# Second attention: score matmuls for the row maxima in the full array shape, between a slot's two score blocks

## The reference

```python
q = (x @ W_dq.T @ W_uq.T).reshape(B, T, nh, hs).transpose(0, 2, 1, 3)   # 16 heads of 8
q_lat = jnp.einsum('bhtd,hdl->bhtl', q, k_eff)
attn = jnp.einsum('bhtl,bsl->bhts', q_lat, c_kv) / math.sqrt(hs)
attn = jnp.where(causal_mask, -jnp.inf, attn)       # key after query: left out
attn = jax.nn.softmax(attn, axis=-1)
ctx = jnp.einsum('bhts,bsl->bhtl', attn, c_kv)
```

## Time and profile before

| what | us |
|---|---|
| three runs, median (lowest, highest) | 2035.82 (2034.11, 2042.33) |
| the profiled execution, first to last instruction (span) | 2036.8 |
| second attention, prelude: first maximum to first score block | 1305.2 to 1337.9 |
| its units 0 to 7, first score block to the end | 1337.9 to 1666 |
| experts of the last layer | 1666 to 2036.8 |

### The profile page before, as it was taken

The page is one execution under the profiler, slowest core; times in us unless marked ns, Lnnn a source line. Parts: engine busy times, 40 slices in busy tenths (PEclk is TensorE's granted clock), DMA queues, the critical chain, the costliest instruction groups (busy, mean ns, idle before and its releaser), DMA issues. The chain is left out here.

```text
span 2036.8 us, 32306 instructions
## 1 busy us (share of the span) xinstructions
PE 1760.2 (86%) x10685; PEld 757.0 (37%) x10685; DVE 1468.9 (72%) x1473; ACT 1323.0 (65%) x2673; POOL 886.3 (44%) x567
## 2 busy tenths in 40 slices
PE   7779999999786777776776699899999999999996
PEld 2313333333344444444443333334444444233332
DVE  3678888887399999999999754556666624465456
ACT  4427777777799999989999534335555553543432
POOL 1076556664299999999999710000000001000000
PEclk8759999999998888888889899879999988999997
DMA  2354444442698888888888411322223000000000
GB/s 108 133 176 162 156 157 151 152 161 110 209 321 315 304 297 312 309 281 314 301 306 300 158 53 48 62 56 56 40 47 58 18 18 0 0 0 0 0 6 16
DMA packets 86546, 288.88 MB, mean 142 GB/s; under 512 B 11671, under 2 KB 15026, under 8 KB 84383
## 3 DMA queue, kind: packets, MB, share of 16 engines
q1 hardware_dynamic: 72319, 236.57, 36.3%
q0 software_dynamic: 13824, 50.34, 6.4%
q10 hardware_dynamic: 288, 0.45, 0.1%
HBM read 214.60 MB, written 61.21 MB: 135 GB/s over the span
## 5 line engine op out<-in xcount | busy, mean ns | idle before, releaser
L565 DVE TENSOR_REDUCE attn_mx<-banks 128x1 f32<-128x1024 f32 (+7 forms) x512 | 501.7, 990 | 148.0 <-PE banks L363 98.4
L1648 POOL TENSOR_TENSOR hc<-st,ct 128x1024 f32<-128x1024 f32 x256 | 597.7, 2368 | 6.4 <-DVE st L1607 6.0
L1607 DVE TENSOR_TENSOR_SCAN st<-da,banks 128x1024 f32<-128x1024 f32 x256 | 562.5, 2266 | 15.6 <-ACT da L1564 6.0
L517 ACT ACTIVATE attn_probs<-banks 128x512 f32<-128x512 f32 (+3 forms) x640 | 307.2, 533 | 193.8 <-PE banks L397 100.2
L1572 ACT ACTIVATE ut<-b_turned,mats 128x128 f32<-128x128 f32 x1024 | 311.6, 387 | 1.7
L1564 ACT ACTIVATE da<-dt,mats 128x1024 f32<-128x1024 f32 x256 | 282.6, 1138 | 25.3 <-DVE st L1607 18.6
L393 PE MATMUL banks<-attn_qa,attn_ka 75*128 75x512 bf16 (+3 forms) x896 | 268.9, 369 | 4.5 <-DMA attn_qa<-attn_mrow 2.5
L1489 PE MATMUL banks<-hc,onecol 128*32 128x512 f32 x1024 | 158.9, 696 | 102.1 <-POOL onecol L1646 79.6
L743 POOL TENSOR_TENSOR made_ahead<-b_turned,x_turned 128x1024 f32<-128x1024 f32 x96 | 183.8, 1914 | 110.9 <-DVE attn_mparts L580 59.1
L361 PE MATMUL banks<-attn_ka,attn_qa 64*128 64x512 bf16 (+3 forms) x512 | 197.1, 385 | 25.1 <-DVE attn_mx L565 21.0
L1465 PE MATMUL banks<-mats,ut 128*128 128x128 f32 x1024 | 162.5, 300 | 45.2 <-DVE st L1607 34.2
(11 more groups left out here) (442 smaller groups left out, 1977.9 us busy)
## 6 DMA issues: line engine op xcount, KB each, us to landing
dt<-dt_rows SPq DMA_DIRECT2D x256, 512.0 KB, 5.5
ahead<-made_ahead POOLq DMA_DIRECT2D x96, 512.0 KB, 3.4
ua<-ahead SPq DMA_DIRECT2D x96, 512.0 KB, 5.9
attn_qa<-q_lin SPq DMA_DIRECT2D x144, 64.0 KB
attn_qu<-attn_qa SPq DMA_DIRECT2D x16, 512.0 KB, 4.3
attn_ka<-k_lin SPq DMA_DIRECT2D x72, 64.0 KB
moe_w<-in_moe_w SPq DMA_DIRECT2D x2, 2048.0 KB, 11.5
mats<-in_mats SPq DMA_DIRECT2D x1, 2876.5 KB, 13.0
```

The source lines that it names most:

```text
L517: nc.scalar.activation(probs[s % 4][:, jj, c0:BLK], scores_exp[jj][:, c0:BLK], ACT.Exp, scale=scale).then_inc(probs_ready, 1)
L565: nc.vector.reduce_max(mx[:, qt, j:j + 1], scores_max[n % 2][:, 0:w], AX.X)\
L1607: nc.vector.tensor_tensor_scan(st[n % 4][:, :], da[n % 4][:, :], pair[:, :, :].rearrange("p h t -> p (h t)"), 0.0, ALU.mult, ALU.add).then ...
L1648: nc.gpsimd.tensor_tensor(hc[n % 8][:, :], st[n % 4][:, :], ct[:, b * SEQ:(b + 1) * SEQ], ALU.mult)\
```

## The change

`qu`, `ku`, the semaphore `mirrored` and the two DMAs of `mirror` fall away for the causal call. `max_unit` takes all 72 rows of `qa` and `ka` for all keys, so that a maximum of more than 512 keys is two matmuls from the same rows; the first one of a unit waits for `loaded` in place of `mirrored`, and so does the load of unit i for the transfers of unit i-2 on the same semaphore. `exp_unit` can make one of its two blocks; in `body` the maxima of place 2s come between the slot's two score blocks. The places, the maxima in them and place 2s+1 stay. The first layer's attention keeps all of this as it was.

```diff
--- before.py
+++ after.py
@@ -159,8 +159,9 @@
     with ExitStack() as ctx:
         qa = [k.sb(f"{tag}_qa{i}", [128, 4, SEQ], BF16, ctx) for i in range(RING)]
         ka = [k.sb(f"{tag}_ka{i}", [128, nk, SEQ], BF16, ctx) for i in range(RING)]
-        qu = [k.sb(f"{tag}_qu{i}", [128, 4, SEQ], BF16, ctx) for i in range(2)]
-        ku = [k.sb(f"{tag}_ku{i}", [128, nk, BLK], BF16, ctx) for i in range(2)]
+        if not causal:
+            qu = [k.sb(f"{tag}_qu{i}", [128, 4, SEQ], BF16, ctx) for i in range(2)]
+            ku = [k.sb(f"{tag}_ku{i}", [128, nk, BLK], BF16, ctx) for i in range(2)]
         probs = [*probs, *(k.sb(f"{tag}_probs{i}", [128, 2, BLK], F32, ctx) for i in range(4 - len(probs)))]
         mx = k.sb(f"{tag}_mx", [128, QT, 4], F32, ctx)
         mneg = k.sb(f"{tag}_mneg", [128, QT, 4], F32, ctx)
@@ -223,7 +224,7 @@
         done_half = [slot_of((1, first_half - 1)), slot_of((0, NM - 1))]
 
         loaded = [k.sem(f"{tag}_loaded{i}") for i in range(2)]
-        mirrored = [k.sem(f"{tag}_mirrored{i}") for i in range(2)]
+        mirrored = None if causal else [k.sem(f"{tag}_mirrored{i}") for i in range(2)]
         const_ready = k.sem(f"{tag}_const")
         ones_set = k.sem(f"{tag}_ones_set")
         ones_in = [k.sem(f"{tag}_ones_in{i}") for i in range(RING)]
@@ -273,6 +274,8 @@
                             .then_inc(ones_in[i], 16)
                     elif p == 0:
                         sp.wait_ge(exp_scored, 2 * NE * (i - RING + 1))
+                    if causal and i >= 2 and p == 0:
+                        sp.wait_ge(loaded[i % 2], 18 * 16 * (i // 2))
                     for j in range(9):
                         if K_ORDER[j] == p:
                             load_k(sp, i, j)
@@ -293,6 +296,8 @@
 
                 def mirror(i):
 
+                    if causal:
+                        return
                     sp.wait_ge(loaded[i % 2], 18 * 16 * (i // 2 + 1))
                     if i >= 2:
                         sp.wait_ge(max_taken, NM * (i - 1))
@@ -346,7 +351,9 @@
 
                 def max_unit(i, n):
                     qt, j, w = max_units[n]
-                    if n == 0:
+                    if n == 0 and causal:
+                        pe.wait_ge(loaded[i % 2], 18 * 16 * (i // 2 + 1))
+                    elif n == 0:
                         pe.wait_ge(mirrored[i % 2], 32 * (i // 2 + 1))
 
                     pe.wait_ge(max_taken, NM * i + max(n - 1, 0))
@@ -354,7 +361,9 @@
                     for lo in range(0, w, BLK):
                         hi = min(lo + BLK, w)
                         diag = causal and hi == w
-                        if lo == 0:
+                        if causal:
+                            lhs, rhs = qa[i % RING][0:ROWS, j, sl(qt, TILE)], ka[i % RING][0:ROWS, kj(j), lo:hi]
+                        elif lo == 0:
                             lhs, rhs = qa[i % RING][0:64, j, sl(qt, TILE)], ka[i % RING][0:64, kj(j), 0:hi]
                         else:
                             lhs, rhs = qu[i % 2][64:128, j, sl(qt, TILE)], ku[i % 2][64:128, kj(j), 0:hi - BLK]
@@ -376,15 +385,15 @@
                                                 ident_b[:, :], start=True, stop=True)
                     last.then_inc(mturned[half], 1)
 
-                def exp_unit(i, s):
+                def exp_unit(i, s, halves=(0, 1)):
                     qb, kt, hp, c0 = exp_units[s]
-                    if s == 0:
+                    if s == 0 and 0 in halves:
                         pe.wait_ge(mrow_sent[0], 48 * (i + 1))
                         if i < RING:
                             pe.wait_ge(ones_in[i], 16)
-                    if s == MID:
+                    if s == MID and 0 in halves:
                         pe.wait_ge(mrow_sent[1], 48 * (i + 1))
-                    for jj in range(2):
+                    for jj in halves:
                         if i > 0 or s > 0:
                             pe.wait_ge(probs_ready, 2 * (NE * i + s) + jj - 1)
                         j = 2 * hp + jj
@@ -455,8 +464,13 @@
                             products_with_v = None
                         if products_with_v:
                             pv_quad(*products_with_v, 0)
-                        first_pass(i, 2 * s)
-                        exp_unit(i, s)
+                        if causal:
+                            exp_unit(i, s, (0,))
+                            first_pass(i, 2 * s)
+                            exp_unit(i, s, (1,))
+                        else:
+                            first_pass(i, 2 * s)
+                            exp_unit(i, s)
                         if s == done_half[1] + 2:
                             turn_max(i, 1)
                         if s == done_half[0] + 2 and i + 1 < UNITS:
```

## The result

| | kernel before | changed kernel |
|---|---|---|
| runs, median (lowest, highest), us | 2035.4 (2034.11, 2042.33), 4 runs | 2017.77 (2014.9, 2020.24), 4 runs |
| span of the profiled execution, us | 2036.8 | 2018.4 (its own time 2020.24) |
| ratio of the times | | 0.9908, 95% interval 0.9878 to 0.9937 |

What follows compares the result with a forecast made beforehand. TensorE was taken to set the pace, with a low-clock stretch in unit 0. Terms -9.0 (units 1 to 6), -7 (unit 0), -1 (prelude), +0.3 (unit 7) gave -16.7 on 2036.8, a 2019 us median; range 2010 to 2031.

Steps and rivals of the forecast that it cites:

- Parts 1 and 2: Units 1 to 6: 51 fewer shape switches save 5.1 us a unit, second-half columns cost 2.2; net 2.9 less.
- part 3: Units 1 to 6: waits take back about 1.4 us a unit, leaving 38.9 each; -9.0 us for six.
- Part 4: Unit 0: clock still falls but recovers after a third to half of the stretch; -7 us (floor -3, ceiling -11).
- Part 6: Unit 7: three 1024-key maxima save 5 switches but pay more columns, and maximum 31 is later; +0.3 us.
- Part 5: Prelude: only some narrow maxima ahead of two front matmuls are on the path; -1 us (0 to -2).
- Part 8: Behind the attention: the experts' instructions are unchanged, though low clock may move; 0 us (-2 to +2).
- Part 7: Mirrors: dropping 16 issues on SyncE's queue costs and gains nothing, hidden by its idle time; 0 us (-0.5 to +0.5).
- A: Rival, unit 0: the low-clock stretch stays as long as now, its term only -3; 2023 us, chance 0.17.
- D: Rival, maxima: shape switches stay, so only the added columns count, 7 x 2.2 us; 2051 us, chance 0.02.
- B: Rival, units 1 to 6: slot 8's chain and VectorE's pace take back nearly all; 2028 us, chance 0.15.
- C: Rival, units 1 to 6: idle TensorE lets the clock fall, 9.5 us a fall; six give 2076; chance 0.10.

Runs made afterwards that it cites:

- 64-row kernel: Changed kernel with the maxima from the first 64 rows alone, for both halves of the keys; 2172.9 us, ratio 1.0687.
- 65-row one: Changed kernel with the maxima from 65 rows instead of 72; 2018.31 us, ratio 0.9891.
- second profile of before: Kernel before, unchanged, in the later of its two further profiles; 2035.78 us.
- first further profile of before: Kernel before, unchanged, profiled once more; 2037.08 us.
- run with the mirrors: Changed kernel with the two mirror copies of each unit issued again and waited for, but not read; 2022.18 us, ratio 0.9924.
- place-only kernel: Kernel before with only the maxima moved between the two score blocks, 64 rows and mirrors kept; 2059.78 us, ratio 1.0103.

## Why the prediction was right, and where a term was off

**Parts 1 and 2 (switches and columns), and part 3 (waits): right.** 38.9 us a unit was forecast, 38.73 measured, -9.9 for six units where -9.0 was forecast. By pieces: the start distances are the predicted ones (0.06 into a maximum, 0.43 for its two blocks of 512), and slots 14 to 17 are each 0.10 shorter (1.59 to 1.49, 1.71 to 1.61). The count of switches is the trace's, 100 and 49, and four single maxima of the 64-row kernel against the 65-row one give the price of a switch afresh, 0.10 us. The net of parts 1 and 2 can be checked roughly too: the 40.39 us of before, less 2.9 net and less the 0.96 of idle time, would be 36.5, and with the long waits taken away a unit takes 36.57 and 36.37, some 0.3 of it still idle ahead of maximum 0.

The waits by size: ahead of maximum 0 1.19 us where 1.3 were forecast (0.2 more than before, not 0.3); ahead of slot 8 0.64 us where 0.8 were; and the 0.2 of slot 10 is gone, since with the order of before the changed shape pays it again (1.34 us against 1.14). The 0.45 for slots 4 and 5 was a little short. From turning out the output to turning the maxima, a stretch with maxima 1 to 5 in both kernels, it is 3.58 us (1424.69 to 1428.27) where it was 3.94 (1435.22 to 1439.16): 0.36 of the 1.0 came, so 0.64 went into waits. Maximum 3 has most of it: it starts 0.52 behind a mask where 0.06 would do. With these sizes the sum closes: 2.9 less 0.2, 0.64 and 0.64, plus the 0.2 of slot 10, is 1.6 us a unit, and 1.66 came. The reading of the earlier trace rows, that this stretch could shrink by 0.34 us at most, held to the hundredth: 3.99 against 3.98.

**Part 4 (unit 0): the clock was rightly named as the source of the gain; its size was wrong.** Its -7 stood for "the clock still falls, and comes back after a third to half". It didn't fall: -12.0, past the ceiling of -11. The ceiling had added 9.5 for the clock and 1.4 for the shape; the second profile of before, where unit 0 ran at full clock, gives 9.7 and, from 40.21 to 37.91, 2.3. The step that failed is the one that took units 1 to 6 as the nearest row for the idle time and let a partly low stretch stand between the bounds. And the premise was incomplete: the low stretch is not unit 0's own, since it can stand in unit 7. Had the profile of before been the one with the full clock in unit 0, this term would have been 2.3 us, and unit 7 would have brought 6.2; that the two profiles compared differ by 12.0 there is in part luck.

**Part 6 (unit 7): a small term lost in the clock.** +0.3 was forecast and -0.9 came, since its low stretch is 6.83 us for 10.24. In the first further profile of before that stretch is 6.83 too, and the unit takes 33.5 us; the two profiles of the changed kernel have 33.5 and 33.9 with a stretch of the same length. The edit itself is worth 0.0 to +0.4, and +0.3 lies in between. Against the second further profile it would be -6.2.

**Part 5 (prelude): right**, -0.8 for -1. **Part 8: nothing to the eye**; +1.6 behind the attention lies within what further profiles show (371.6 and 373.9 us for the kernel before, against 372.3; 372.0 for the changed one, against 373.9). **Part 7 (mirrors): off by little.** "Cost and gain nothing" was wrong by 0.13 us a unit (0.8 in all, past its bound of 0.5), and the falls of the clock in the same run may or may not be theirs. The cover that the prediction named, SyncE's idle time, was there; the cost came through the wait ahead of slot 8 all the same.

The forecast for the span was -16.7 and -18.4 came. Unit 0 brought 5.0 more than its term, unit 7 1.2 and units 1 to 6 0.9; 3.6 us ahead of the maxima and 1.6 behind the attention went the other way, with 0.2 in the prelude. So 2019 is as close to 2017.8 as it is partly because two errors met.

**The rivals.** A (the low stretch stays) fell: no profile with 72 rows has one in unit 0. D (only the columns count) fell by the start distances: a maximum of 1024 keys and its way in and out cost 0.15 + 0.32 + 0.16 us in the paired shape and 0.06 + 0.43 + 0.15 in the full one, the same; one of 128 keys saves the two switches. The Trainium skill, "TensorEngine Tiling (Array Packing)", says under "Theoretical Speedup" up to twice the rate for a short contraction, and under "Key Properties" that a change of the mode drains the engine. The trace agrees with both, the second half being free in the pair and the drain costing 0.10 us each way. B (waits take back nearly all) was half right: its waits are there, but they took back about the 1.4 us a unit that the forecast had put on them, not all. C (the clock falls in units 1 to 6) did not come in either profile of the changed kernel, and its mechanism is real: falls at just the idle time that it named. In the full shape, in the run with the mirrors and in the one with 65 rows, they cost 1.0 to 1.4 us each, not 9.5; with 64 rows in the old pairs one cost 10.8 (unit 4 of the place-only kernel), about the price that C gave.

What stays open: whether the short falls in the two full-shape runs come from what was changed in them or from chance; what in the 64-row shape keeps the clock low, the unused half or the changes of shape; and why the mirrors lengthen the issue of the rows' DMAs.

## What to carry to other kernels

Read what a small matmul costs from the distance of starts, not from its duration: where neighbours differ in the part of the array they use, each change costs 0.10 us, and using more rows than the job needs can be the cheaper way. When TensorE gets faster, list what it now arrives at too soon; here three waits of 0.3 to 1.2 us held 2.2 us a unit, 0.96 of it there before the change; moving one maximum and one turning by a slot each gave that back. When two orders of the same work are compared by slots, take boundaries between which both have the same work; here those were the second score blocks, since the first ones have a maximum more or less between them. A gain that comes through the clock shows in only some executions at a given place, so take a second profile of the kernel before, before a difference in one unit is credited to that unit.

## What the runs showed of the hardware that was not expected

- **A shape of 64 rows next to full shapes, with half of the array unused in it, kept the granted clock at 0.50 (1.2 GHz) for 246 us**, though TensorE was busy for 242.5 of them, and for 75 us later on. With 65 rows the clock came back 3.4 us after each of the four falls in units 1 to 6. Each of these six falls came within about 1 us of the same idle time, 1.18 to 1.19 us ahead of a maximum of 128 columns. It is a matter of how often and not a strict rule: with 64 rows one fall of four in units 0 to 6 lasted only 3.4 us too (unit 1).
- **The paired 64-row shape of the kernel before sits between the two**: one long low stretch of 23.9 to 27.3 us in each of three profiles, in unit 0 or in unit 7, and none in the 18 units 1 to 6 of the three. With the maxima between the blocks, it has three falls in one profile, of 27.3, 3.4 and 27.3 us.
- **The step from 64 to 65 rows is the whole difference in pace at full clock**: 65 and 72 rows give the same 38.73 us a unit at full clock, and four single maxima are 0.82 us shorter than with 64.
- **Two changes that are each supposed to help need not add**: the place is worth 0.0 us in the full shape and costs 1.1 us a unit, and in the one profile taken more low clock, in the half shape.
